# A vision-transformer block on one core: queries of the last tokens as columns, turning by DMA, and three smaller edits

## The reference, cut to what matters

```python
# x holds the complex coefficients C of 32 images: the state-space kernel gives 128 rows of 1024 for each
h = 2.0 * einsum('chn,hnl->chl', Cc, exp(dtA[:, :, None] * ell)).real
h = concatenate([broadcast_to(cls_tok, ...), h], axis=1)     # 129 tokens: the class token in front
n = layernorm(h)
q, k, v = n @ Wq.T, n @ Wk.T, n @ Wv.T         # 32 query heads, 8 key/value heads, 32 wide; q and k get rotary positions
attn = softmax(causal(q @ k.T / sqrt(32)))      # within an image
h = h + (attn @ v) @ Wo.T
x_q = fake_quant_per_token(layernorm(h))        # 8 bits: scale = max|x| / 127, round, clip
w_q = fake_quant_per_channel(w)
out = h + einsum('bsi,oi->bso', x_q, w_q) + b
```

## Time and profile before

| | us |
|---|---|
| median of three runs | 1524.17 (1523.65 to 1526.39) |
| the profiled execution | 1532.89 |
| its span | 1531.1 |
| mix stage, about | 0 to 163 |
| start of attention (tiles -2 and -1), about | 163 to 196 |
| attention, tile 0 on | 196 to 1013 |
| passage to the output stage | 950 to 1050 |
| output stage | 1013 to 1531 |

### The profile page before, as it was taken

How to read it: one execution, slowest core, us unless ns; L and a number is a source line. 1 busy time by engine, 2 the same in 40 slices (tenths; PEclk the granted TensorE clock), 3 DMA queues, 4 the chain that set the end, 5 groups by cost and what they waited for, 6 DMA issues and landing times. The chain is left out here.

```text
span 1531.1 us, 34469 instructions
## 1 busy us (share of the span) xinstructions
PE 1460.7 (95%) x10770; PEld 1137.7 (74%) x10802; DVE 1300.4 (85%) x2350; ACT 770.0 (50%) x2710; POOL 823.6 (54%) x794
## 2 busy tenths in 40 slices
PE   5999899999999999999999999679999999999997
PEld 3999787777777777777777777457677777777774
DVE  7888689889999998999999998659988888888885
ACT  6896466666676767667676676531111111111110
POOL 5795136667676776767667676313333333333332
PEclk9999999999999999999999999779999999999999
DMA  9466536667767777677776776853333232333321
GB/s 234 108 145 149 155 94 177 178 191 209 212 192 199 201 201 213 193 204 200 198 210 198 208 196 176 277 165 127 114 96 121 85 123 92 114 104 101 115 78 48
DMA packets 220106, 244.90 MB, mean 160 GB/s; under 512 B 30001, under 2 KB 158130, under 8 KB 220050
## 3 DMA queue, kind: packets, MB, share of 16 engines
q1 hardware_dynamic: 214290, 223.14, 51.2%
q10 hardware_dynamic: 5760, 21.04, 4.6%
HBM read 138.29 MB, written 106.57 MB: 160 GB/s over the span
## 5 line engine op out<-in xcount | busy, mean ns | idle before, releaser
L1209 ACT ACTIVATE pr<-sm,ml 128x128 f32<-128x128 f32 x1024 | 399.0, 393 | 157.4 <-DVE ml L1385 157.3
L965 POOL TENSOR_TENSOR pr<-pr,ri 128x512 f32<-128x512 f32 x256 | 266.8, 1042 | 223.6 <-DVE ri L1392 217.7
L1060 PE MATMUL att_ps<-w_lo,xT_hi 128*128 128x512 f32 x792 | 326.1, 412 | 0.0
L1060 PE MATMUL att_ps<-w_hi,xT_hi 128*128 128x512 f32 x792 | 318.9, 403 | 0.0
L1060 PE MATMUL att_ps<-w_hi,xT_lo 128*128 128x512 f32 x792 | 313.7, 396 | 0.0
L1673 PE MATMUL ffn_o<-wo_hi,cT_hi 128*128 128x512 f32 x528 | 216.5, 410 | 2.8 <-ACT wo_hi L1703 2.8
L1376 DVE TENSOR_TENSOR sm<-att_ps,cst 128x512 f32<-128x512 f32 x256 | 170.0, 664 | 52.9 <-PE att_ps L1121 52.9
L1673 PE MATMUL ffn_o<-wo_hi,cT_lo 128*128 128x512 f32 x528 | 207.3, 393 | 0.0
L1673 PE MATMUL ffn_o<-wo_lo,cT_hi 128*128 128x512 f32 x528 | 206.4, 391 | 0.0
L1209 ACT ACTIVATION_READ_ACCUMULATOR pr<-sm,ml 128x1 f32 x1024 | 193.6, 189 | 0.0
L1369 DVE STREAM_TRANSPOSE pB<-pr 128x512 f32<-128x512 f32 x256 | 176.2, 688 | 20.2 <-DMA p_blocks<-pB 19.8
(11 more groups left out here) (209 smaller groups left out, 2409.8 us busy)
## 6 DMA issues: line engine op xcount, KB each, us to landing
pT<-p_blocks SPq DMA_DIRECT2D x256, 256.0 KB, 2.9
p_blocks<-pB SPq DMA_DIRECT2D x512, 64.0 KB, 2.0
h_rows<-ho SPq DMA_DIRECT2D x64, 256.0 KB, 4.0
ctx_turned<-ctxo SPq DMA_DIRECT2D x64, 256.0 KB, 3.5
h_in<-h_rows SPq DMA_DIRECT2D x32, 512.0 KB, 4.5
out_dram<-yo SPq DMA_DIRECT2D x32, 512.0 KB, 2.7
ctx_in<-ctx_turned SPq DMA_DIRECT2D x30, 512.0 KB, 3.6
hbuf<-h_rows ACTq DMA_DIRECT2D x29, 512.0 KB, 4.8
```

The source lines that it names most:

```text
L965: G.tensor_tensor(pr[:, g % 4], pr[:, g % 4], ri[:, g % 2, :].unsqueeze(2).to_broadcast([P, GQ, P]), ALU.mult).then_inc(p_ready, 1)
L1060: mm = nc.tensor.matmul(bank[:], x_part[:, t[1], e, tok:tok + P], w_part[blk][:, e, :], start=(r == 0), stop=(r == EC * 3 - 1))
L1209: a = nc.scalar.activation(pr[:, g % 4, q, :], sm[:, g % 2, q, :], ACT.Exp, bias=ml[:, b[1], 0, h:h + 1], accum_out=ml[:, b[1], 1, h:h + 1])
```

## The change

- The last tokens' queries. Tile -1 projects block 0 alone (24 matmuls, 6 a step in four steps). The last token's q of every image is row 127 of its own tile's queries; GpSimd copies this column from `qT` into `q_end` (now 8 x 32 columns) twice a tile (`save_q`), ScalarE's `store_q` waits for it, and TensorE turns `q_end` once at the start of the output stage (`turn_q_end`). `end_scores` reads the result from PSUM.
- Turning by DMA. `turn_w` and `turn_xq` leave TensorE, their copies leave ScalarE. SyncE issues one DMA with `transpose=True` for each 128x1024 bf16 block, eight for w and one for every tile's xq.
- The orders around it. On SyncE the load of h follows the wait for xq. In tile -1 the statistics of tile 0 come in step 0, GpSimd normalises tile 0 ahead of its loop, the first `round_w` goes to step 7 behind `split_x`, the `quantise_w` of tile 0 to steps 3, 5 and 7, and the first rounds of tile -2 to step 1.
- The store of the last rows' context goes from tile 3 to tile 30 of the output stage.
- `hb` is computed in two halves, the first after `f_xn`, the second after `xq`.
- 6 and 6 matmuls of zeros in place of 5 and 3.

```diff
-    WARM_TURNS = (5, 3)
+    WARM_TURNS = 6
...
         if at(t, -2):
-            return {0: range(8, 12), 2: range(12, 14), 5: range(14, 16), 7: range(16, 18)}.get(s, ())
+            return {1: range(8, 12), 2: range(12, 14), 5: range(14, 16), 7: range(16, 18)}.get(s, ())
...
         if at(t, -1):
-            return {5: 0}.get(s)
+            return {7: 0}.get(s)
...
-            return {2: (2, 3), 4: (4, 5), 7: (6, 7)}.get(s, ())
+            return {3: (2, 3), 5: (4, 5), 7: (6, 7)}.get(s, ())
...
+        def turn_w(u):
+            sp.wait_ge(quantised, u + 1)
+            sp.dma_start(wq8[:, :, u * P:(u + 1) * P], wq[:, u % 2, :], transpose=True).then_inc(w_turned[u % 2], 16)
...
             if at(t, 0):
+                turn_w(0)
+                turn_w(1)
                 load_w_pair(2)
+                turn_w(2)
+                turn_w(3)
                 load_w_pair(3)
+                turn_w(4)
+                turn_w(5)
                 no_later_keys()
...
+        def save_q(b, half):
+            pool.wait_ge(q_stored, 2 * number(b) + half + 1)
+            G.tensor_copy(q_end[:, GQ * half:GQ * half + GQ, bass.ds(number(b), 1)], qT[:, half, :, P - 1:P]
+                          ).then_inc(q_saved, 1)
...
             if at(t, -1):
-                pool.wait_ge(xn_ready, XROUNDS)
+                inverse_deviation(n)
+                normalise(n, 0)
+                normalise(n, 1)
+                rope_sum(t, 0)
                 G.memset(c_end[:], 0.0).then_inc(c_end_zero, 1)
+                return
...
-            per_step = NBLK * EC * 3 // STEPS
+            per_step = EC * 3 // 4 if last_rows(t) else NBLK * EC * 3 // STEPS
+            count = EC * 3 if last_rows(t) else NBLK * EC * 3
...
-                if s == 1 and has_rows(n):
+                if s == 0 and (last_rows(n) or at(n, 0)):
+                    statistics(n)
...
+                if s == 1 and has_rows(n) and not last_rows(n) and not at(n, 0):
                     statistics(n)
...
+        def turn_xq(c):
+            sp.dma_start(xqT[:, c[1]], xq[:, c[1], :], transpose=True).then_inc(xq_turned[c[1]], 16)
+
         def body(t):
+            if at(t, NB - 2):
+                sp.wait_ge(end_ready, 1)
+                sp.dma_start(tail_dram[0:NB], ctx_end[0:NB]).then_inc(rest_out, 16)
             if exists(shifted(t, 2), NT):
                 load_ctx(sp, shifted(t, 2))
+            c = shifted(t, -1)
+            if exists(c, NT):
+                sp.wait_ge(xq_ready, number(c) + 1)
+                if not fixed(c) or number(c) >= 2:
+                    sp.wait_ge(dense, 2 * number(c) - 2)
             if exists(shifted(t, 1), NT) and not at(t, 0):
                 load_h(sp, shifted(t, 1))
+            if exists(c, NT):
+                turn_xq(c)
             if exists(shifted(t, -2), NT):
                 store(shifted(t, -2))
...
-                nc.gpsimd.tensor_tensor(hb[:, t[1], :], h1[:, t[1], :], bias_sb[:], ALU.add).then_inc(biased, 1)
+                for half in range(2):
+                    cols = slice(half * BK, (half + 1) * BK)
+                    if half == 0:
+                        pool.wait_ge(normed, u + 1)
+                    else:
+                        pool.wait_ge(xq_ready, u + 1)
+                    done = nc.gpsimd.tensor_tensor(hb[:, t[1], cols], h1[:, t[1], cols], bias_sb[:, cols], ALU.add)
+                done.then_inc(biased, 1)
...
+        def turn_q_end():
+
+            pe.wait_ge(q_saved, 2 * NB)
+            for c in range(EC):
+                mm = nc.tensor.transpose(C_BANK[c // 4][0:NB, (c % 4) * P:(c % 4 + 1) * P], q_end[:, c, :], ident)
+            mm.then_inc(q_end_turned, 1)
...
             if half == 0:
-                pe.wait_ge(xq_stored, u + 1)
+                pe.wait_ge(xq_turned[c[1]], TURN_COUNT * (c[0] + 1))
...
             if exists(t, NT) and not at(t, 0):
-                project(pe, t, 0, PER_HALF)
-            if exists(c, NT) and not at(t, 1):
-                turn_xq(c)
-            if exists(t, NT) and not at(t, 0):
-                project(pe, t, PER_HALF, 2 * PER_HALF)
-            if at(t, 1):
-                turn_xq(c)
+                project(pe, t, 0, 2 * PER_HALF)
...
+            if at(t, 0):
+                turn_q_end()
```

More of the change, by code:

```diff
@@ L942, in rope_sum @@
             rows = slice(0, NB if last_rows(t) else P)
-            pool.wait_ge(rot_ready, NBLK * nth(t) + blk + 1)
+            pool.wait_ge(rot_ready, NBLK * nth(t) + (NBLK if last_rows(t) else blk + 1))
             if last_rows(t):
-                dst = k_end[rows] if blk == 0 else q_end[rows, (blk - 1) * BK:blk * BK]
+                dst = k_end[rows]
             elif blk == 0:
@@ L951, in rope_sum @@
                 dst = rsq[:]
-            G.tensor_tensor(dst, ra[rows, 0:cols], rb[rows, 0:cols], ALU.add).then_inc(rope_ready, 1)
+            G.tensor_tensor(dst, ra[rows, 0:cols], rb[rows, 0:cols], ALU.add
+                            ).then_inc(rope_ready, NBLK if last_rows(t) else 1)
         def normalise(n, r):
+            if at(n, 0) and r == 0:
+                pool.wait_ge(rstd_ready, nth(n) + 1)
+                pool.wait_ge(x_turned, 2 * nth(n))
             cols = slice(r * BK, (r + 1) * BK)
@@ L990, in body @@
                     normalise_p(d, g)
-                if s == 1 and has_rows(b):
+                if s == 1 and has_rows(b) and not last_rows(b):
                     rope_sum(b, 2)
@@ L1002, in body @@
                     save_ctx(c, 0)
+                if s == 1 and exists(b, NB):
+                    save_q(b, 0)
+                if s == 4 and exists(b, NB):
+                    save_q(b, 1)
                 if s == 5 and has_rows(n) and not last_rows(n):
@@ L1045, in project @@
                 if r == 0:
-                    at_least(pe, rot_ready, q - 1)
+                    if not (at(t, 0) and blk == 0):
+                        at_least(pe, rot_ready, q - 1)
                     if blk == 2:
                         pe.wait_ge(v_stored, nth(t) + 1)
+                    if at(t, 0) and blk == 1:
+                        pe.wait_ge(v_stored, 1)
                     if last_rows(t):
-                        done = EC * (blk + 1) + (XROUNDS if blk > 0 else 0)
-                        pe.wait_ge(hi_done, done)
-                        pe.wait_ge(lo_done, done)
+                        pe.wait_ge(hi_done, R_MIX + XROUNDS)
+                        pe.wait_ge(lo_done, R_MIX + XROUNDS)
+                    if at(t, 0) and blk > 0:
+                        pe.wait_ge(hi_done, R_ALL - EC * (2 - blk))
+                        pe.wait_ge(lo_done, R_ALL - EC * (2 - blk))
                 if blk == 0 and r in (0, EC * 3 // 2):
@@ L1094, in turn_x @@
             mm.then_inc(x_turned, 1)
-        def turn_w(u):
-            pe.wait_ge(quantised, u + 1)
-            if u == 0:
-                pe.wait_ge(hi_done, R_ALL)
-                pe.wait_ge(lo_done, R_ALL)
-            if u < 6:
-                at_least(pe, w_stored, u - 3)
-            else:
-                pe.wait_ge(x_lo, 2 * nth((0, 1)) + 2)
-                pe.wait_ge(w_stored, u)
-            bank = w_bank(u)[:].bitcast(BF16)
-            for i in range(EC):
-                mm = nc.tensor.transpose(bank[:, i * P:(i + 1) * P], wq[:, u % 2, i * P:(i + 1) * P], ident_b[:])
-            mm.then_inc(w_turned, 1)
         def scores(b, half):
@@ L1115, in scores @@
             pe.wait_ge(k_stored, number(b) + 1)
-            if at(b, 0) and half == 0:
-                pe.wait_ge(w_stored, 6)
             for q in range(GQ):
@@ L1126, in weigh @@
             u = number(b)
-            if at(b, 0) and half == 0:
-                pe.wait_ge(w_stored, EC)
             pe.wait_ge(p_whole[half], 64 * (u + 1))
@@ L1150, in body @@
                 if has_rows(t):
-                    project(t, s * per_step, s * per_step + ahead)
+                    project(t, min(s * per_step, count), min(s * per_step + ahead, count))
                 if s == 0 and exists(b, NB):
@@ L1165, in body @@
                     pe_round(pe, r)
-                for u in w_turns_at(t, s):
-                    turn_w(u)
                 if has_rows(t):
-                    project(t, s * per_step + ahead, (s + 1) * per_step)
+                    project(t, min(s * per_step + ahead, count), min((s + 1) * per_step, count))
                 if at(t, NB):
@@ L1433, in body @@
                     normalise_last_rows(n)
-                if s == 6 and has_rows(t):
+                if s == 6 and has_rows(t) and not last_rows(t):
                     rotate(t, 1)
+                if s == 7 and has_rows(n):
+                    split_x(n, 1)
                 i = w_round_at(t, s)
@@ L1482, in ffn_stage @@
     PER_HALF = 3 * EC
+    TURN_COUNT = 16
     def sem(name):
@@ L1788, in tensor @@
         pe.wait_ge(masked, 8 * NB)
+        for i in range(2):
+            pe.wait_ge(shared["w_turned"][i], 8 * EC)
         iterations(pe, body)
```

91 lines of the change are left out of this document (34 added, 57 removed).

## The result

The changed kernel takes **1504.54 us** (median of 4 runs, 1501.16 to 1508.96) against 1524.72 for the kernel before (4 runs, 1523.65 to 1526.39): a ratio of 0.986, 95% interval 0.9833 to 0.9887. The forecast was 1502.5, with a range of 1494 to 1534. Run again later beside 9 runs of the kernel before (median 1528.43), it took 1505.84, ratio 0.9856 (0.9833 to 0.9879). Both profiled executions are slower than the median of their kernel (1508.96 against 1504.54, 1532.89 against 1524.72), so pieces taken from the pair sum to 23.9, and the medians differ by 20.2.

A forecast was written before the change was run, and what follows sets the result against it. TensorE was taken to bound both 32-tile loops. Terms -16.1 - 7.4 - 0.9 + 1.4 + 1.0 - 1.1 + 1.3 sum to -21.8 on the profile, -21.7 on the median 1524.17: 1502.5 us, range 1494 to 1534.

The forecast's parts named there:

- The loop: Output loop: turning xq by DMA takes 0.52 us a tile off TensorE, over 31 tiles -16.1 us.
- L: Output loop: time from xq being ready to its DMA-turned copy having landed, taken as 5.9 us.
- slack: Output loop: time from xq being ready to the dense layer that reads it, read as 7.95 us.
- The rival of a late turning: Output loop: xq's turning lands late, TensorE waits before each dense layer; about 1559 us at L = 11; chance 0.17.
- The start: Start of attention: tile 0 begins 8.6 us earlier, tile 1 7.4 earlier; -7.4 us booked for the end.
- the split behind it: Start of attention: fewer TensorE matmuls in tile -1 allow tile 0's earlier start; VectorE's rounds of weights set tile 1's.
- The w turnings: Attention tiles 0 and 1: w turned by DMA; nothing gained in tile 0, 16 turnings saved in tile 1, -0.9 us.
- Warm matmuls: Before the mix stage: 6 and 6 in place of 5 and 3 make the g turnings end later, +1.4 us.
- Waits of tiles 3 and 4: Output loop: TensorE's waits for xq in these tiles go as VectorE is relieved, -1.1 us.
- Dense layer 0: Beginning of the output loop: waits about as long for the DMA as for the copy, 0, between -1 and +4.
- Last tile: End of the output loop: whole DMA exposed, 4.0 in place of 2.1 us, less 0.6 from hb: +1.3 us.
- The context store: Output loop: moving it to tile 30 removes SyncE's wait at tile 3, where TensorE waits for no loads: 0.

The follow-up runs named there:

- e1: The changed kernel with xq turned on TensorE again and copied by ScalarE, all else kept: 1525.27 us, ratio 0.9986 to the kernel before.
- e5: The changed kernel with both halves of hb added right after rstd in all tiles but the last: 1508.26 us, ratio 0.9881.
- e4_chain_2: The changed kernel with the load of h in two pieces, each issued after the previous landed, the turning of xq behind them: 1510.09 us, ratio 0.9888.
- e4_chain_4: The changed kernel with the load of h in four pieces, each issued after the previous landed, the turning of xq behind them: 1590.68 us, one run.
- e3: The changed kernel with 48 unread matmuls put back on TensorE in tile -1: 1514.81 us, ratio 0.9915.
- e9: The changed kernel with attention's start put back: 48 unread matmuls in tile -1, w turned on TensorE, first rounding at step 5: 1508.26 us, ratio 0.9864.
- e6: The changed kernel with 5 and 3 warm matmuls in place of 6 and 6: 1504.8 us, ratio 0.9853.
- e10: The changed kernel with the store of the last rows' context back at tile 3, with its wait: 1519.29 us, one run.

## Why the prediction was right

*The loop: right, and the mechanism too.* -16.1 was forecast for 31 tiles at 0.52; measured 0.556, which is 17.2. e1 takes it back whole. L was 5.05 against 5.9 taken, slack 7.7 against 7.95, f_xn 0.81 in every tile. e5, e4_chain_2 and e4_chain_4 show the slack of the steady loop from both sides; before dense layer 0 it is smaller. The rival of a late turning was priced right in its wait and too low in its time, since the clock behind a wait was left out.

*The start: tile 0 and 1 near, the end wrong.* -8.6 was forecast for tile 0 (it came to -10.2, 9.5 of it after tile -1's start) and -7.4 for tile 1 (-5.9). That the number for tile 1 came near is luck, since e3 refutes the split behind it: TensorE's 48 matmuls alone move tile 1 by 9.7. The step that failed for the end is the one after it: that the end gains what tile 1 gains. Between tile 1 and tile 7 VectorE is behind, TensorE runs dry, and by e9 0 to 3 us are left. -8.3 was booked for the start (with the w turnings), so it gave some 5 to 8 us less. The w turnings, -0.9, were no gain: what their cover cost, a slow transfer that holds ScalarE's half of wq and SyncE's queue, stood in my bounds ("3 to 4 us late") but not in the value.

*Other terms.* Warm matmuls: +1.4 forecast, -0.7 in the one pair of profiles, not told from 0 by e6. The term took the clock's return at 39.9, as in the kernel before; it came at 36.7, and the second turnings of g ended at 39.8 and not after 41. Waits of tiles 3 and 4: -1.1, right. Dense layer 0: 0 forecast, -1.3 came, as nothing waits there now. The passage gave -1.2 with q_end's turning (1.03) in it, but eight profiles of the same passage differ by 3.7 us, so nothing can be said of its terms. Last tile: +1.3 forecast, +0.6 from its rstd to the end; the DMA took 3.1 from xq's end to the dense layer, where 4.0 was taken.

*The context store: the number right, the reason not enough.* 0 held against the kernel before, and e10 shows that without this edit the change would have lost 8.7 us. I had looked at who waits for SyncE before the change and not at who would after it.

*The sum* came within 2 us (-21.7 forecast, -20.2 on the medians) because misses cancelled: the loop and dense layer 0 gave 2.4 more, the warm matmuls showed no cost, passage and last tile came out 2.9 better in the one pair of profiles, and the start gave some 5 to 8 less. That the total is so close is luck; what was right by its mechanism is the loop, which is nearly all of the gain.

## What to carry to other kernels

Work taken off the engine that bounds a steady loop is paid in full, tile by tile; an earlier start is worth only what is left once the next engine's backlog is worked off, so follow a landmark some tiles into the steady loop before booking it. When a queue takes over an urgent transfer, list every wait on that queue again: one that was free can now cost a tile. And price a wait on TensorE with the slower stretch behind it.
